# A fourth subtract level in the rounding chains of an SSM and ternary feed-forward layer

## The chip, the cores and the metric

The kernel runs on one Trainium2 chip, on 8 cores. Each core computes one of the 8 sequences of the batch with the same program and its own input; the cores exchange nothing. The time is the device time of the slowest core, in microseconds (us); lower is better. Engines are named as the profile names them: PE is TensorE, DVE is VectorE, ACT is ScalarE, POOL is GpSimd, SP is SyncE.

## The reference

For every sequence x of 4096 positions and 1024 features, the layer is, cut to what matters:

```python
u   = rmsnorm(layernorm(x));  Bu = u @ B_w.T            # 256 states
h_t = lam * h_(t-1) + Bu_t;   y  = h @ C_w.T + D_skip * u
a   = layernorm(x) + y;       z  = rmsnorm(a)
x   = x + a + (silu(z @ w1.T) * (z @ w3.T)) @ w2.T      # 2736 wide

def act_quant(v):                                       # per position
    scale = 127.0 / max(max(abs(v)), 1e-5)
    return clip(round(v * scale), -128, 127) / scale
def bitlinear(v, w, b):                                 # w in {-1, 0, 1} / scale
    return act_quant(rmsnorm2(v)) @ weight_quant(w).T + b
h   = gelu(bitlinear(layernorm(x), f1, b1))             # 4096 wide
x   = x + bitlinear(h, f2, b2)
```

What the change touches is the `round` in `act_quant`, once for the 1024 features that enter the first ternary product and once for the 4096 that enter the second.

## The kernel before, in words

Features lie on the partitions and positions along the free axis. A tile is 256 positions (TT), so a core has 16 tiles. Each phase goes over all 16 tiles.

**The order of the work.** There is no scheduler. `ctx.op` appends an instruction to its engine's list in the order in which the Python code runs, and works out which semaphore values it must wait for from the names that it reads and writes. Each engine takes its own list strictly in that order. An instruction that reads what the one before it on the same engine wrote waits for that engine's own semaphore too, so the instructions of a rounding chain come one after the other.

**First phase** (`p1_...`). Per tile: `p1_A` loads x and computes the statistics and the scan (L270 to L333). `p1_B` computes the state output and the second norm, and ends with the S1 tile (L374). `p1_CD` does the gated feed-forward: 22 slices with 8 matmuls for the gate (L390) and 8 for the value (L396), in three PSUM tiles PaA, PaB and PaC that are used in turn. ACT computes silu (L401) and DVE multiplies (L404), which frees two PSUM tiles; then 176 matmuls with w2 (L411). `p1_E` adds, stores the result to DRAM and computes the scale of `act_quant`. `p1_y1s` multiplies by it (L520). `p1_F` rounds, in 8 chunks of 128x256, and stores each chunk to DRAM (L548, L550). The loop runs `p1_CD(it)`, `p1_A(it+1)`, `p1_E(it)`, `p1_y1s(it)`, `p1_B(it+1)`, `p1_F(it)`. So on DVE the rounding of tile `it` lies behind the S1 tile of tile `it+1`, and ahead of the L404 multiplies of `it+1`.

**Weights.** Behind a barrier, the two ternary weight matrices are read twice from DRAM: once for the mean of their absolute values (L600 to L612), once to be made -1, 0 or 1 in bf16 (L650 to L664).

**Second phase** (`p2_...`). Per tile, column group by column group (fc, 32 of 128 columns): 8 matmuls into one of two PSUM tiles (L716), a multiplication by DVE that reads them (L723), GELU by ACT into HHT (L726), the square by ACT (L732), one matmul that sums the squares (L735), and two DVE instructions for the running maximum (L746, L749). `p2_stats` turns sum and maximum into the scale. `p2_quant_pair(it, g)` scales and rounds two column groups at a time, in 128x512 (L805 to L828), into HQT. `p2_m7_mms` does the 256 matmuls of the second product from HQT (L836), `p2_m7_evac` finishes the tile. The loop interleaves two tiles: for each pair g, DVE rounds pair g of tile `it`, and then the column groups 2g and 2g+1 of tile `it+1` are computed. The second product of tile `it-1` is put on PE ahead of that loop, and so is, for all tiles but the last, the broadcast of the next tile's scale into IABC (L152 on PE, L155 on DVE, called at L698), which DVE takes ahead of pair 0.

**The rounding chain.** DVE converts to int32 and back (L809, L811 and L529, L531) and subtracts, which leaves the fractional difference d (L813, L533). Then 4.0 is added (L816, L536), and for each s of 4, 2 and 1 a mask "d > s - 0.5" is computed (L820, L540) and s times the mask is subtracted (L824, L544). What is left is subtracted from the value (L828, L548). `round_chain` (L157) holds a third copy of the chain, but nothing calls it.

Of the kernel before, what the change touches and what calls it, by code (L numbers as in the profile page):

```python
# [106 lines left out]
def build(T=4096, TT=256):  # L107
# [38 lines left out]
           f=lambda e: e.dma_start(out=IDF[:], in_=identd[:]))  # L146
# [10 lines left out]
    def round_chain(src_ap, src_keys, iq, kiq, dbuf, kd, mask_ap, kmask, emit_out):  # L157
        ctx.op("dve", r=list(src_keys), w=[kiq],
               f=lambda e: e.tensor_copy(out=iq, in_=src_ap))
        ctx.op("dve", r=list(src_keys) + [kiq], w=[kd],  # L160
               f=lambda e: e.scalar_tensor_tensor(out=dbuf, in0=iq, scalar=-1.0,
                                                  in1=src_ap, op0=ALU.mult, op1=ALU.add))
        ctx.op("dve", r=[kd], w=[kd],
               f=lambda e: e.tensor_scalar(out=dbuf, in0=dbuf, scalar1=4.0,
                                           scalar2=None, op0=ALU.add))
        for s in (4.0, 2.0, 1.0):
            ctx.op("dve", r=[kd], w=[kmask],
                   f=lambda e, s=s: e.tensor_scalar(out=mask_ap, in0=dbuf,
                                                    scalar1=s - 0.5, scalar2=None,
                                                    op0=ALU.is_gt))  # L170
            ctx.op("dve", r=[kd, kmask], w=[kd],
                   f=lambda e, s=s: e.scalar_tensor_tensor(out=dbuf, in0=mask_ap,
                                                           scalar=-s, in1=dbuf,
                                                           op0=ALU.mult, op1=ALU.add))
        emit_out()
# [347 lines left out]
    def p1_F(it):  # L523
        t0 = it * TT
        X = X0 if it % 2 == 0 else X1
        kX = "X%d" % (it % 2)
        for c in range(NCHUNK):
            ctx.op("dve", r=[kX], w=["XI1"],
                   f=lambda e, c=c, X=X: e.tensor_copy(out=XI1[:], in_=X[:, c, :]))  # L529
            ctx.op("dve", r=["XI1"], w=["DHP"],  # L530
                   f=lambda e: e.tensor_copy(out=DHP[:], in_=XI1[:]))  # L531
            ctx.op("dve", r=[kX, "DHP"], w=["DHP"],
                   f=lambda e, c=c, X=X: e.tensor_tensor(out=DHP[:], in0=X[:, c, :],  # L533
                                                         in1=DHP[:], op=ALU.subtract))
            ctx.op("dve", r=["DHP"], w=["DHP"],
                   f=lambda e: e.tensor_scalar(out=DHP[:], in0=DHP[:], scalar1=4.0,  # L536
                                               scalar2=None, op0=ALU.add))
            for s in (4.0, 2.0, 1.0):
                ctx.op("dve", r=["DHP"], w=["MHP"],
                       f=lambda e, s=s: e.tensor_scalar(out=MHP[:], in0=DHP[:],  # L540
                                                        scalar1=s - 0.5, scalar2=None,
                                                        op0=ALU.is_gt))
                ctx.op("dve", r=["DHP", "MHP"], w=["DHP"],
                       f=lambda e, s=s: e.scalar_tensor_tensor(out=DHP[:], in0=MHP[:],  # L544
                                                               scalar=-s, in1=DHP[:],
                                                               op0=ALU.mult, op1=ALU.add))
            ctx.op("dve", r=[kX, "DHP"], w=["XQS"],
                   f=lambda e, c=c, X=X: e.tensor_tensor(out=XQS[:], in0=X[:, c, :],  # L548
                                                         in1=DHP[:], op=ALU.subtract))
            ctx.op("sp", r=["XQS"], w=["xqh"], dma="xq",  # L550
                   f=lambda e, c=c, t0=t0: e.dma_start(
                       out=xqh[c * 128:(c + 1) * 128, t0:t0 + TT], in_=XQS[:]))
# [248 lines left out]
    def p2_quant_pair(it, g):  # L801
# [11 lines left out]
               f=lambda e: e.tensor_tensor(out=DH[:], in0=Y1H[:], in1=DH[:],  # L813
                                           op=ALU.subtract))
        ctx.op("dve", r=["DH"], w=["DH"],
               f=lambda e: e.tensor_scalar(out=DH[:], in0=DH[:], scalar1=4.0,  # L816
                                           scalar2=None, op0=ALU.add))
        for s in (4.0, 2.0, 1.0):
            ctx.op("dve", r=["DH"], w=["MH"],
                   f=lambda e, s=s: e.tensor_scalar(out=MH[:], in0=DH[:],  # L820
                                                    scalar1=s - 0.5, scalar2=None,
                                                    op0=ALU.is_gt))
            ctx.op("dve", r=["DH", "MH"], w=["DH"],
                   f=lambda e, s=s: e.scalar_tensor_tensor(out=DH[:], in0=MH[:],  # L824
                                                           scalar=-s, in1=DH[:],
                                                           op0=ALU.mult, op1=ALU.add))
# [125 lines left out]
```

How the kernel before makes its waits and increments, by code:

```python
            def body(e):  # L892
                for o in ops:
                    for s, v in o.waits:
                        e.wait_ge(sem[s], v)
                    if o.emit is not None:
                        instr = o.emit(e)
                        instr.then_inc(sem[o.sem], o.inc)
```

## Time and profile before

| What | Value |
|---|---|
| Time, median of 2 runs | 7898.35 us (7889.26 to 7907.43) |
| The profiled execution | 7907.0 us |
| Its span on the slowest core, core 1 | 7905.4 us |
| Spans of the 8 cores | 7877.9 to 7905.4 us |
| DVE busy | 3924.4 us in 8881 instructions |
| PE busy | 3167.4 us in 19024 matmuls |
| ACT busy | 865.6 us in 1563 instructions |

The profile records one execution; its span is the time from the first to the last instruction of a core, and the execution's own time lies 1.6 us above it. Busy time is the sum over an engine's instructions. Idle time is counted ahead of an instruction and put down to what released it. The granted clock of PE is given as a share of 2.4 GHz.

### The profile page before, as it was taken

What the parts mean: (1) busy time and instruction counts of PE and PEld (TensorE: products, weight loads), DVE (VectorE), ACT (ScalarE), POOL (GpSimd) and SP (SyncE); (2) the same over time, 40 slices, a digit from 0 to 9 for tenths busy, and PEclk for the clock granted to TensorE, in tenths of its full rate; (3) what the DMA queues carried; (4) which work ended last, traced back from release to release, by engine and by line L of the source; (5) the groups of instructions that cost most, each with busy time, mean ns of one, the idle gap of its engine ahead of it and who ended that gap; (6) DMA issues with size and microseconds to landing.
All of it is one profiled execution on the core that took longest, in us unless ns stands there. A gap on an engine that the chain in (4) does not pass through costs nothing.

```text
span 7905.4 us, 65940 instructions; the slowest of 8 cores (7877.9 to 7905.4 us)
## 1 busy us (share of the span) xinstructions
PE 3167.4 (40%) x19024; PEld 2061.8 (26%) x19024; DVE 3924.4 (50%) x8881; ACT 865.6 (11%) x1563; POOL 5.1 (0%) x8
## 2 busy tenths in 40 slices
PE   3444444444444443300443444344443444344433
PEld 2333333333333332100221222122222222122212
DVE  2444454455445555443445544554455444544465
ACT  1000000001000000000211111111111111111110
POOL 0000000000000000000000000000000000000000
PEclk8666666666666666555555555555555555555556
DMA  6000000000000000522000000000000000000000
GB/s 105 14 14 14 14 14 14 14 14 18 15 14 14 14 14 11 171 106 74 8 1 14 14 14 0 14 14 14 9 5 14 14 14 1 14 14 14 1 11 11
DMA packets 120946, 173.91 MB, mean 22 GB/s; under 512 B 5748, under 2 KB 105236, under 8 KB 118548
## 3 DMA queue, kind: packets, MB, share of 16 engines
q1 hardware_dynamic: 115412, 152.20, 6.0%
q0 software_dynamic: 5184, 17.50, 1.4%
q8 instruction: 164, 2.69, 0.1%
q14 instruction: 186, 1.52, 0.1%
HBM read 145.22 MB, written 41.96 MB: 24 GB/s over the span
## 4 chain that ended last, share of the span: by engine, by line
DVE 44%; PE 30%; issue 12%; ACT 7%; DMA 5%; DVEq 2%; ACTq 0%; SPq 0%
DVE DH L824 7%; PE psH L716 6%; PE psO L836 6%; PE psF L411 4%; ACT HHT L726 4%; DVE MH L820 3%; DVE PR L723 3%; DMA WQ<-f2T 3%; DVE DHP L544 2%; DVEq L895 2%; PE psRow L260 2%; ACT HS L732 2%; PE PaC L152 1%; PE PaB L390 1%; PE PaA L390 1%
## 5 line engine op out<-in xcount | busy, mean ns | idle before, releaser
L735 PE MATMUL psRowH<-HS,ONEB 128*1 128x256 bf16 x512 | 190.1, 371 | 2223.9 <-ACT HS L732 2223.9
L716 PE MATMUL psH<-XQ,f1q 128*128 128x256 bf16 x4096 | 954.4, 414 | 10.8 <-DVE IABC L155 10.8
L735 PEld LDWEIGHTS psRowH<-HS,ONEB 128*1 128x1 bf16 x512 | 40.5, 79 | 2451.9 <-issue 2451.9
L716 PEld LDWEIGHTS psH<-XQ,f1q 128*128 128x128 bf16 x4096 | 525.8, 139 | 335.5 <-issue 148.1
L726 ACT ACTIVATE HHT<-PR,B1S,THR 128x256 f16<-128x256 f32 x512 | 306.8, 599 | 2621.2 <-DVE PR L723 2621.0
L824 DVE SCALAR_TENSOR_TENSOR DH<-MH,DH 128x512 f16<-128x512 f16 x768 | 531.6, 692 | 82.9 <-DVE MH L820 4.3
L836 PE MATMUL psO<-HQT,f2q 128*128 128x256 bf16 x4096 | 495.4, 285 | 119.1 <-DVE HQT L828 109.5
L723 DVE TENSOR_TENSOR PR<-psH,IABC 128x256 f32<-128x256 f32 x512 | 215.6, 421 | 593.8 <-PE psH L716 593.7
L836 PEld LDWEIGHTS psO<-HQT,f2q 128*128 128x128 bf16 x4096 | 412.7, 102 | 207.5 <-issue 145.3
L411 PE MATMUL psF<-GV,w2sb 128*128 128x256 bf16 (+1 forms) x2816 | 350.2, 279 | 21.3 <-DVE GV L404 11.8
L746 DVE TENSOR_TENSOR MX<-MX,HHT 128x256 f16<-128x256 f16 x496 | 145.3, 293 | 417.7 <-ACT HHT L726 417.7
L390 PE MATMUL PaB<-S1b,w1sb 128*128 128x256 bf16 x896 | 129.8, 293 | 484.3 <-DVE GV L404 484.3
L411 PEld LDWEIGHTS psF<-GV,w2sb 128*128 128x128 bf16 (+1 forms) x2816 | 270.2, 99 | 102.7 <-issue 63.9
L152 PE MATMUL PaC<-ROWS,ONESR 1*128 1x256 f32 x224 | 132.9, 694 | 353.0 <-DVE ROWS L310 113.3
L820 DVE TENSOR_SCALAR MH<-DH 128x512 f16<-128x512 f16 x768 | 225.9, 294 | 84.3 <-DVE DH L824 2.3
L749 DVE SCALAR_TENSOR_TENSOR MX<-HHT,MX 128x256 f16<-128x256 f16 x496 | 211.0, 425 | 53.0 <-DVE MX L746 1.9
L155 DVE CAST IABC<-psH 128x256 f16<-128x256 f32 x16 | 6.8, 425 | 452.5 <-PE psH L152 452.5
L152 PE MATMUL psH<-ROW,ONESR 1*128 1x256 f32 x96 | 50.0, 615 | 440.7 <-DMA ROW<-iah 363.6
L390 PEld LDWEIGHTS PaB<-S1b,w1sb 128*128 128x128 bf16 x896 | 91.9, 104 | 503.4 <-issue 488.2
L732 ACT ACTIVATE HS<-HHT 128x256 bf16<-128x256 f16 x512 | 213.2, 416 | 76.4 <-ACT HHT L726 2.1
L390 PE MATMUL PaA<-S1b,w1sb 128*128 128x256 bf16 (+1 forms) x1024 | 157.4, 305 | 89.1 <-DVE XI L529 83.4
L287 DVE TENSOR_SCALAR ROWS<-psRow 1x256 f32<-1x256 f32 x16 | 6.6, 412 | 362.0 <-PE psRow L260 362.0
(162 smaller groups left out, 4623.7 us busy)
## 6 DMA issues: line engine op xcount, KB each, us to landing
WQ<-f1T SPq DMA_DIRECT2D x16, 2048.0 KB, 7.8
WQ<-f2T SPq DMA_DIRECT2D x64, 512.0 KB, 3.5
X<-xT SPq DMA_DIRECT2D x16, 1024.0 KB, 5.7
xoh<-XOUT SPq DMA_DIRECT2D x16, 1024.0 KB, 4.4
XO<-xoh SPq DMA_DIRECT2D x16, 1024.0 KB, 8.6
outT<-FIN SPq DMA_DIRECT2D x16, 1024.0 KB, 5.6
xqh<-XQS SPq DMA_DIRECT2D x128, 64.0 KB, 1.6
XQ<-xqh SPq DMA_DIRECT2D x16, 512.0 KB, 9.5
```

The source lines that it names most:

```text
L152: f=lambda e: e.matmul(pgrp[:, 0:TT], ONESR[:], row_ap, start=True, stop=True))
L390: mm = e.matmul(pg[0:fsz, :], w1sb[:, c, off:off + fsz], S1[:, c, :], start=(c == 0), stop=(c == NCHUNK - 1))
L411: mm = e.matmul(psF[:, dc, :], w2sb[0:fsz, fs, dc * 128:(dc + 1) * 128], GV[0:fsz, fs, :], start=(fs == 0), stop=(fs == 21))
L716: mm = e.matmul(pH[:], f1q[:, c, fc * 128:(fc + 1) * 128], XQ[:, c, :], start=(c == 0), stop=(c == NCHUNK - 1))
L723: f=lambda e, pH=pH, PR=PR: e.tensor_tensor(out=PR[:], in0=pH[:], in1=IABC[:], op=ALU.mult))
L726: f=lambda e, fc=fc, PR=PR: e.activation(out=HHT[:, fc, :], in_=PR[:], func=AF.Gelu, bias=B1S[:, fc:fc + 1], scale=THR[:, 4:5]))
L732: f=lambda e, fc=fc, hsq=hsq: e.activation(out=hsq[:], in_=HHT[:, fc, :], func=AF.Square))
L735: f=lambda e, fc=fc, hsq=hsq: e.matmul(psRowH[:, 0, :], ONEB[:], hsq[:], start=(fc == 0), stop=(fc == F2CHUNK - 1)))
L749: f=lambda e, fc=fc: e.scalar_tensor_tensor(out=MX2[:], in0=HHT[:, fc, :], scalar=-1.0, in1=MX2[:], op0=ALU.mult, op1=ALU.max))
L820: f=lambda e, s=s: e.tensor_scalar(out=MH[:], in0=DH[:], scalar1=s - 0.5, scalar2=None, op0=ALU.is_gt))
L824: f=lambda e, s=s: e.scalar_tensor_tensor(out=DH[:], in0=MH[:], scalar=-s, in1=DH[:], op0=ALU.mult, op1=ALU.add))
L836: mm = e.matmul(psO[:, dc, :], f2q[0:128, fc, dc * 128:(dc + 1) * 128], HQT[:, fc, :], start=(fc == 0), stop=(fc == F2CHUNK - 1))
```

## The change

The rounding chain starts from 8.0 instead of 4.0, and has four levels (8, 4, 2, 1) instead of three. Each chain gets two DVE instructions more: a compare and a scalar_tensor_tensor. The edit stands in three places.

```diff
@@ round_chain
-               f=lambda e: e.tensor_scalar(out=dbuf, in0=dbuf, scalar1=4.0,
+               f=lambda e: e.tensor_scalar(out=dbuf, in0=dbuf, scalar1=8.0,
                                            scalar2=None, op0=ALU.add))
-        for s in (4.0, 2.0, 1.0):
+        for s in (8.0, 4.0, 2.0, 1.0):
...
@@ p1_F
-                   f=lambda e: e.tensor_scalar(out=DHP[:], in0=DHP[:], scalar1=4.0,
+                   f=lambda e: e.tensor_scalar(out=DHP[:], in0=DHP[:], scalar1=8.0,
                                                scalar2=None, op0=ALU.add))
-            for s in (4.0, 2.0, 1.0):
+            for s in (8.0, 4.0, 2.0, 1.0):
                 ctx.op("dve", r=["DHP"], w=["MHP"],
                        f=lambda e, s=s: e.tensor_scalar(out=MHP[:], in0=DHP[:],
                                                         scalar1=s - 0.5, scalar2=None,
...
@@ p2_quant_pair
-               f=lambda e: e.tensor_scalar(out=DH[:], in0=DH[:], scalar1=4.0,
+               f=lambda e: e.tensor_scalar(out=DH[:], in0=DH[:], scalar1=8.0,
                                            scalar2=None, op0=ALU.add))
-        for s in (4.0, 2.0, 1.0):
+        for s in (8.0, 4.0, 2.0, 1.0):
             ctx.op("dve", r=["DH"], w=["MH"],
                    f=lambda e, s=s: e.tensor_scalar(out=MH[:], in0=DH[:],
                                                     scalar1=s - 0.5, scalar2=None,
```

The order of DVE changes in two places; that of the other engines doesn't. In the second phase, DVE's list for the rounding of one pair and what follows it stood so before (DH holds the difference, MH the mask, HQT the rounded value, psH0 the PSUM tile of the next tile's column group):

```order
L813 TENSOR_TENSOR DH<-Y1H,DH 128x512 [waits dve]
L816 TENSOR_SCALAR DH<-DH 128x512 [waits dve]
L820 TENSOR_SCALAR MH<-DH 128x512 [waits dve]
L824 SCALAR_TENSOR_TENSOR DH<-MH,DH 128x512 [waits dve]
L820 TENSOR_SCALAR MH<-DH 128x512 [waits dve]
L824 SCALAR_TENSOR_TENSOR DH<-MH,DH 128x512 [waits dve]
L820 TENSOR_SCALAR MH<-DH 128x512 [waits dve]
L824 SCALAR_TENSOR_TENSOR DH<-MH,DH 128x512 [waits dve]
L828 TENSOR_TENSOR HQT<-Y1H,DH 128x512 [waits dve]
L723 TENSOR_TENSOR PR0<-psH0,IABC 128x256 [waits pe]
```

And so stands DVE's list at the same place of the changed kernel:

```order
L813 TENSOR_TENSOR DH<-Y1H,DH 128x512 [waits dve]
L816 TENSOR_SCALAR DH<-DH 128x512 [waits dve]
L820 TENSOR_SCALAR MH<-DH 128x512 [waits dve]
L824 SCALAR_TENSOR_TENSOR DH<-MH,DH 128x512 [waits dve]
L820 TENSOR_SCALAR MH<-DH 128x512 [waits dve]
L824 SCALAR_TENSOR_TENSOR DH<-MH,DH 128x512 [waits dve]
L820 TENSOR_SCALAR MH<-DH 128x512 [waits dve]
L824 SCALAR_TENSOR_TENSOR DH<-MH,DH 128x512 [waits dve]
L820 TENSOR_SCALAR MH<-DH 128x512 [waits dve]
L824 SCALAR_TENSOR_TENSOR DH<-MH,DH 128x512 [waits dve]
L828 TENSOR_TENSOR HQT<-Y1H,DH 128x512 [waits dve]
L723 TENSOR_TENSOR PR0<-psH0,IABC 128x256 [waits pe]
```

One compare and one scalar_tensor_tensor stand between the difference and the rounded value, and the read of the PSUM tile is two instructions further down.

In the first phase, DVE's list for one chunk of p1_F stood so before (XI1 is the int32 value, DHP the difference, MHP the mask, XQS the rounded chunk):

```order
L529 CAST XI1<-X0 128x256
L531 CAST DHP<-XI1 128x256
L533 TENSOR_TENSOR DHP<-X0,DHP 128x256
L536 TENSOR_SCALAR DHP<-DHP 128x256
L540 TENSOR_SCALAR MHP<-DHP 128x256
L544 SCALAR_TENSOR_TENSOR DHP<-MHP,DHP 128x256
L540 TENSOR_SCALAR MHP<-DHP 128x256
L544 SCALAR_TENSOR_TENSOR DHP<-MHP,DHP 128x256
L540 TENSOR_SCALAR MHP<-DHP 128x256
L544 SCALAR_TENSOR_TENSOR DHP<-MHP,DHP 128x256
```

In the changed kernel DVE has at this place:

```order
L529 CAST XI1<-X0 128x256
L531 CAST DHP<-XI1 128x256
L533 TENSOR_TENSOR DHP<-X0,DHP 128x256
L536 TENSOR_SCALAR DHP<-DHP 128x256
L540 TENSOR_SCALAR MHP<-DHP 128x256
L544 SCALAR_TENSOR_TENSOR DHP<-MHP,DHP 128x256
L540 TENSOR_SCALAR MHP<-DHP 128x256
L544 SCALAR_TENSOR_TENSOR DHP<-MHP,DHP 128x256
L540 TENSOR_SCALAR MHP<-DHP 128x256
L544 SCALAR_TENSOR_TENSOR DHP<-MHP,DHP 128x256
L540 TENSOR_SCALAR MHP<-DHP 128x256
L544 SCALAR_TENSOR_TENSOR DHP<-MHP,DHP 128x256
```

Here too each chunk is two instructions longer. DVE's list has 768 rows more in all: 2 for each of the 128 chunks of the first phase and of the 256 pairs of the second.

## Rows read from the trace of the kernel before

**Rows 1.** The page, part 1 (busy us, share, instructions); the spans and clocks by core.

```profile
PE 3167.4 (40%) x19024; PEld 2061.8 (26%) x19024; DVE 3924.4 (50%) x8881; ACT 865.6 (11%) x1563; POOL 5.1 (0%) x8
...
core 1: 7905.4 us, clock 0.604
...
core 4: 7877.9 us, clock 0.607
```

**Rows 2.** Windows of core 1: busy us (instructions) by engine, PEclk, DMA share, GB/s.

```profile
0.00:3180.00 3180.00, 1430.89 (x9904) 1027.82 (x9904) 1526.78 (x3607) 297.88 (x491) 5.15 (x8) 0.68 0.08 20
...
3870.00:7878.00 4008.00, 1583.63 (x8398) 954.09 (x8399) 2112.75 (x4988) 532.21 (x1005) 0.00 (x0) 0.56 0.03 10
```

**Rows 3.** The page, part 4: the chain that ended last.

```profile
DVE 44%; PE 30%; issue 12%; ACT 7%; DMA 5%; DVEq 2%; ACTq 0%; SPq 0%
DVE DH L824 7%; PE psH L716 6%; PE psO L836 6%; PE psF L411 4%; ACT HHT L726 4%; DVE MH L820 3%; DVE PR L723 3%; DMA WQ<-f2T 3%; DVE DHP L544 2%; DVEq L895 2%; PE psRow L260 2%; ACT HS L732 2%; PE PaC L152 1%; PE PaB L390 1%; PE PaA L390 1%
```

**Rows 4.** Groups of DVE: busy us, mean ns | idle us before, releasers.

```profile
L824 DVE SCALAR_TENSOR_TENSOR DH<-MH,DH 128x512 f16<-128x512 f16 x768 | 531.6, 692 | 82.9 <-DVE MH L820 4.3
L820 DVE TENSOR_SCALAR MH<-DH 128x512 f16<-128x512 f16 x768 | 225.9, 294 | 84.3 <-DVE DH L824 2.3 <-DVE DH L816 1.7
...
L544 DVE SCALAR_TENSOR_TENSOR DHP<-MHP,DHP 128x256 f16<-128x256 f16 x384 | 163.3, 425 | 42.2 <-DVE MHP L540 2.6
...
L540 DVE TENSOR_SCALAR MHP<-DHP 128x256 f16<-128x256 f16 x384 | 87.2, 227 | 43.3 <-DVE DHP L544 2.3 <-DVE DHP L536 0.9
```

**Rows 5.** Waits: who waited for whom, us in total, times, longest us.

```profile
PE psRowH L735 <- ACT HS L732: 2223.9, 512, 15.5
...
DVE PR L723 <- PE psH L716: 593.7, 272, 2.6
...
PE PaB L390 <- DVE GV L404: 484.3, 15, 33.3
...
DVE IABC L155 <- PE psH L152: 452.5, 16, 32.0
```

**Rows 6.** Timeline of one pair, second phase: start, us, instruction, idle before.

```profile
5088.06 0.42 DVE L723 TENSOR_TENSOR PR<-psH,IABC 128x256 f32<-128x256 f32 x1
...
5094.54 1.89 PE L716 MATMUL psH<-XQ,f1q 128*128 128x256 bf16 x8
...
5097.24 0.69 DVE L824 SCALAR_TENSOR_TENSOR DH<-MH,DH 128x512 f16<-128x512 f16 x1
5098.04 0.29 DVE L820 TENSOR_SCALAR MH<-DH 128x512 f16<-128x512 f16 x1
5098.44 0.69 DVE L824 SCALAR_TENSOR_TENSOR DH<-MH,DH 128x512 f16<-128x512 f16 x1
...
5100.43 0.42 DVE L828 TENSOR_TENSOR HQT<-Y1H,DH 128x512 bf16<-128x512 f16 x1
5100.77 0.42 DVE L723 TENSOR_TENSOR PR<-psH,IABC 128x256 f32<-128x256 f32 x1
...
5103.00 1.89 PE L716 MATMUL psH<-XQ,f1q 128*128 128x256 bf16 x8
```

**Rows 7.** Timeline of DVE, pair 0 of the last tile, second phase.

```profile
7731.43 0.69 DVE L824 SCALAR_TENSOR_TENSOR DH<-MH,DH 128x512 f16<-128x512 f16 x1
7757.14 0.42 DVE L828 TENSOR_TENSOR HQT<-Y1H,DH 128x512 bf16<-128x512 f16 x1 [25.02 <-PE psO L836]
```

**Rows 8.** Windows, first phase: L411 in two tiles, and the chain of p1_F.

```profile
2306.00:2332.00 26.00, 25.40 (x180) 18.55 (x181) 0.94 (x1) 1.22 (x1) 0.00 (x0) 0.81 0.00 1
...
2882.00:2904.00 22.00, 21.40 (x179) 16.80 (x180) 0.99 (x1) 1.28 (x1) 0.00 (x0) 1.00 0.01 1
...
2996.00:3034.00 38.00, 5.37 (x34) 3.94 (x33) 28.68 (x89) 2.05 (x3) 0.00 (x0) 0.59 0.04 13
```

**Rows 9.** L836 on the timeline, and the window of the pairs behind it.

```profile
5131.53 5.81 PE L836 MATMUL psO<-HQT,f2q 128*128 128x256 bf16 x32
5137.49 7.15 PE L836 MATMUL psO<-HQT,f2q 128*128 128x256 bf16 x64
...
5167.00:5391.00 224.00, 72.03 (x289) 36.19 (x290) 131.81 (x311) 35.48 (x67) 0.00 (x0) 0.50 0.04 12
```

## Prediction

> **What bounds the kernel now.** I read the page first, for the busy shares [rows 1]: VectorE (DVE) is busy for 3924.4 us of a span of 7905.4, TensorE for 3167.4. Neither is near full, so the shares alone name no bound. The stage windows [rows 2] split the span into three parts: the first phase (16 tiles, 0 to 3180 us), the weight passes, and the second phase (16 tiles, 3870 to 7878 us). The chain that ended last [rows 3] gives 44% of the span to DVE and 30% to TensorE, and its largest line is L824, one of the two instructions that the change adds: the engines take turns, and time added in a DVE turn counts in full unless TensorE would have been the later one there. So the question is who waits for whom around the two rounding chains.
>
> In the second phase, the timeline of one pair of column groups [rows 6] answers it. TensorE does the next 8 matmuls of L716 from 5094.54 to 5096.43 us, beneath the DVE chain. DVE goes through its three levels and starts L828 only at 5100.43. The read of that PSUM tile (L723) follows at 5100.77 with no wait, since the matmuls had been done for 4.3 us. Only the second chunk's matmuls, 5103.00 to 5104.89, make DVE wait, and they can't start before the first chunk has gone through L723, GELU and square, all behind the chain. The waits say the same for all tiles [rows 5]: DVE waits at L723 for TensorE 272 times, so for about one chunk of each pair; TensorE waits for the square (L735 behind L732) for 2223.9 us in all. The rounding chain is in series with everything else in the pair.
>
> In the first phase, the chain of lines 529 to 548 stands on DVE ahead of the L404 multiplies of the next tile. TensorE fills its three PSUM tiles and then stands still until the first L404 frees one: 484.3 us in 15 waits, 32.3 us each [rows 5]. The window from 2996 to 3034 us shows that stretch, with TensorE busy for 5.37 of 38 us [rows 8]. So this chain is in series too.
>
> **The change, part by part.** The constant 4.0 that becomes 8.0 changes no instruction's shape, and costs nothing. Each chain gets a fourth level: one compare (L820 or L540) and one scalar_tensor_tensor (L824 or L544), with operands and shapes that the trace already has three times per chain. The edit of round_chain is in a function that nothing calls. So no price is unknown; each is read from the same lines [rows 4]. Since every one of these instructions waits for the one before it on its own engine, the idle time ahead of them belongs to the price.
>
> - Second phase, one level over 128x512 f16: L824 takes 531.6 us busy and 82.9 idle, L820 takes 225.9 busy and 84.3 idle, 924.7 us over 768 of each, 1.204 us. The timeline agrees: from one L824 to the next it is 1.20 us [rows 6]. There are 16 tiles with 16 pairs, 256 levels more.
> - Of these 256, one is covered. In tile 15 no input of a next tile is loaded, so DVE starts pair 0 at once, and L828 then waits 25.02 us for the 256 matmuls of the tile before, which read the buffer that it writes [rows 7]. In the other tiles DVE waits for those matmuls ahead of the chain, at the cast of IABC (452.5 us in 16 waits [rows 5]), so pair 0's chain comes after them and is exposed. 255 x 1.204 = 307.0 us.
> - First phase, one level over 128x256 f16: (163.3 + 42.2 + 87.2 + 43.3) / 384 = 0.875 us. 16 tiles with 8 chunks: 128 x 0.875 = 112.0 us. All of it is exposed, the last tile too, where a barrier stands behind the chain. The DMA that empties XQS, a single buffer, gets more time from one chunk to the next with the fourth level, not less.
>
> At these two places the Trainium skill has a rule on the gap. Measured: L820 starts 0.80 us behind the start of an L824 that takes 0.69, a gap of 0.11 [rows 6]. "VectorE: DVE Perf Modes", section "The DRAIN you can't avoid", puts a pipeline flush of about the operation's duration less 266 ns behind each operation. With the means of rows 4 a level of 512 would then take 294 + 28 + 692 + 426 = 1440 ns, one of 256 would take 227 + 425 + 159 = 811 ns, and the change would cost 367 + 104 = 471 us. The trace doesn't bear the rule out for this pair, and the measured gap decides.
>
> The sum is 307.0 + 112.0 = 419.0 us. The profiled execution took 7907.0 us for a span of 7905.4, so it would become 8326. It lies 8.65 us above the median of the runs, 7898.35; I forecast from the median: 7898.35 + 419.0 = 8317 us, 5.3% more.
>
> Two things can move this beside the added work, and both are TensorE's clock. First, its cold start. In the 256 matmuls of a tile (L836) the first 32 take 5.81 us where 64 take 7.15 later [rows 9], so 5.81 - 3.58 = 2.2 us are lost before it has risen to 2.4 GHz. Each tile of either phase has one such start, 32 in all, and I take the first phase's for as dear. The longer tiles shift where the clock rises. If the loss vanished or doubled in all of them it would be 70 us less or more; but as some tiles will gain where others lose, I take 0, and 10 us to each side. Beyond that a longer DVE stretch can't cool TensorE: it is at 0.50 (1.2 GHz) all through the pairs already [rows 9]. Second, a level between the two. The 176 matmuls of L411 fill a window of 22 us at granted clock 1.00 (2.4 GHz), and one of 26 us at 0.81 [rows 8]. Core 1, the slowest, shows it; between the slowest and the fastest core lie 27.5 us at otherwise equal work [rows 1]. I take no change, with 27 us to each side as the far ends. Of an instruction stream that grows by 768 of DVE's 8881 instructions, the means in rows 4 already hold the occasional longer gap (1.204 against the usual 1.20).
>
> **Rivals.**
> 1. The 0.81 level goes. TensorE rests longer between its dense blocks, so whatever brings 0.81 may come less often. The slowest core would then be like the fastest: 8317 - 27 = 8290 us. For it: the stretches at 0.81 are all in dense blocks of the first phase. Against it: the dense blocks themselves are as long as before. The Trainium skill, "TensorE: Matmul & The Clock Gate", has such a level of 13/16 as a peak-current limit when three cores of a die run dense matmuls (section "Seeing it yourself"); 0.81 in rows 8 agrees with it, and by it the level would come back in the same blocks, so that the time stays at the forecast. Chance of rival 1: 0.05. The mirror of it, more tiles at 0.81, costs 4 us per tile in L411; in 13 tiles more it would be 52 us, 8369 us. Chance 0.03.
> 2. Only the second phase pays. If TensorE's three blocks ahead of the stall in the first phase grew or DVE's chain ended before TensorE needs it, 112 us would be hidden: 7898 + 307 = 8205 us. Against it stand the 32.3 us of wait per tile, which the chain would have to lose before it were covered. Chance 0.02.
> 3. Not slower. The place is the pair loop and the mechanism TensorE as the later one: the added level lies beneath the matmuls of the next chunk, and L723 starts as before. It decides as soon as those matmuls end later than L828 does, which needs 4.3 us more of them, over three times their 1.89. With the first phase beneath its matmuls too, the time stays at 7898 us. The idle 50% of DVE speaks for it at first sight; that L723 starts directly behind L828 in rows 6 speaks against it. Chance 0.02.
> 4. The change doesn't do what it says, if the compiled program drops or merges a level. Against it: the order of the changed kernel holds 768 more DVE rows, and four compares in each chain. The time would be 7898 us; its chance is counted with rival 3.
>
> **How the numbers follow.** The forecast as worked out has 0.87. With 10 us for cold starts and part of the 27 us of the 0.81 level its own range is 8295 to 8341, and I give that as the whole range: what is left out (rivals 2 to 4, the far parts of rival 1, an error of mine in the sum) is under 2 in 10. A measurement of this kernel can tell about 2% from no change, 158 us. Slower by over 2%: the forecast and rivals 1 and 2, 0.97. Within 2%: rivals 3 and 4, 0.02. Faster by over 2%: nothing in the rows gives it, 0.01.
>
> **What would show it right or wrong.** In the profile of the changed kernel L820 and L824 should have 1024 instructions each at 294 and 692 ns, L540 and L544 512 each at 227 and 425 ns, DVE busy for 3924.4 + 256 x 0.986 + 128 x 0.652 = 4260 us, and TensorE's busy time unchanged. The wait of PE PaB L390 for L404 should grow from 32.3 to about 39 us, that of L828 for psO should shrink from 25.0 to 23.8 us, and a pair should take 1.2 us more than its 12.7 (from L723 at 5088.06 to L723 at 5100.77 in rows 6). The waits of L723 for TensorE should stay at 272 times and 594 us. If they shrink by much, the chain was covered in part (rivals 2 and 3). If the added gaps are longer than 0.11 us, the price per level was wrong. If the added lines fit and the total doesn't, it is the clock: the windows of L411 and L836 would show it.

## The result, and the profile after

The changed kernel takes 8358.44 us (median of 11 runs, 8336.40 to 8404.92). Beside it the kernel before takes 7910.09 us (median of 10, 7886.50 to 7927.98). The ratio is 1.0579, with a 95% interval from 1.0555 to 1.0603. An execution in which one die is over 1% longer than the other at a lower granted clock is left out of the median times below (8019.84 us in experiment 5, 7553.66 us in experiment 12). The forecast was 8317 us in a range from 8295 to 8341, so the direction and the main term held, but the time lies 17 us above the range. Of the 41 us between forecast and result, 12 lie in the base (two runs had a median of 7898.35, ten have 7910.09). The other 29 lie in the difference: 448 us, where 419 were forecast.

Part 1 of the page of the changed kernel, slowest core, answers to [rows 1]:

```profile
PE 3216.3 (38%) x19024; PEld 2085.4 (25%) x19024; DVE 4261.8 (51%) x9649; ACT 865.6 (10%) x1563; POOL 5.2 (0%) x8
```

DVE has its 768 instructions more and is busy for 4261.8 us, against the 4260 worked out. TensorE is busy for 49 us more, with the same instructions: that is already a sign of its clock.

The groups of DVE on core 4 of the changed kernel (busy us, mean ns | idle us before) answer to [rows 4]:

```profile
L824 DVE SCALAR_TENSOR_TENSOR DH<-MH,DH 128x512 f16<-128x512 f16 x1024 | 709.0, 692 | 112.0 <-DVE MH L820 7.7
L820 DVE TENSOR_SCALAR MH<-DH 128x512 f16<-128x512 f16 x1024 | 300.9, 294 | 112.0 <-DVE DH L824 3.7 <-DVE DH L816 0.9
L544 DVE SCALAR_TENSOR_TENSOR DHP<-MHP,DHP 128x256 f16<-128x256 f16 x512 | 217.7, 425 | 56.2 <-DVE MHP L540 3.4
...
L540 DVE TENSOR_SCALAR MHP<-DHP 128x256 f16<-128x256 f16 x512 | 116.2, 227 | 56.9 <-DVE DHP L544 2.8 <-DVE DHP L536 0.5
```

A level costs (709.0 + 112.0 + 300.9 + 112.0) / 1024 = 1.205 us in the second phase and (217.7 + 56.2 + 116.2 + 56.9) / 512 = 0.873 us in the first. The forecast had 1.204 and 0.875.

The waits on the slowest core, core 3, answer to [rows 5] (us in total, times, longest us):

```profile
PE psRowH L735 <- ACT HS L732: 2514.9, 512, 16.7
...
DVE PR L723 <- PE psH L716: 594.1, 272, 2.6
...
PE PaB L390 <- DVE GV L404: 582.5, 15, 39.6
...
DVE IABC L155 <- PE psH L152: 451.9, 16, 32.3
```

DVE's wait at L723 is what it was, 272 times and 594 us, so nothing of the added levels was absorbed there. TensorE waits 582.5 / 15 = 38.8 us per tile for the first L404 instead of 32.3; the forecast was about 39. The one covered pair shows too. In the timeline of core 4, pair 0 of the last tile, the wait of [rows 7] is 24.17 us long instead of 25.02. The forecast was 23.8, 1.2 us less:

```profile
8151.87 0.43 DVE L828 TENSOR_TENSOR HQT<-Y1H,DH 128x512 bf16<-128x512 f16 x1 [24.17 <-PE psO L836]
```

So the missing 29 us are not in the chains. To find them, compare cores whose TensorE clock was hardly ever at 0.81. Core 4 of the changed kernel has 11 us at 0.81, and in experiment 1, the kernel before once more, core 4 has none. These are the windows of core 4 of the changed kernel, cut at its stages: the first phase, the weight pass for the mean (first L603 to the end of the last), the pass that makes the ternary weights (first L654 to the end of the last L662), and the second phase. The first number behind the stretch is its length in us, then busy us by engine, PEclk, DMA share, GB/s:

```profile
88.60:3251.30 3162.70, 1411.67 (x9888) 1018.37 (x9888) 1609.93 (x3856) 292.08 (x481) 0.82 (x1) 0.67 0.06 15
3264.20:3458.60 194.40, 59.78 (x252) 26.54 (x252) 75.49 (x43) 0.00 (x0) 0.00 (x0) 0.54 0.49 162
3473.80:3823.10 349.30, 0.00 (x0) 0.00 (x0) 160.37 (x120) 0.00 (x0) 0.00 (x0) 0.50 0.27 90
3831.10:8314.50 4483.40, 1675.57 (x8854) 1006.76 (x8854) 2411.68 (x5615) 567.83 (x1072) 0.00 (x0) 0.56 0.03 9
```

The same stages on core 4 of the kernel before, in experiment 1:

```profile
91.10:3141.30 3050.20, 1409.62 (x9888) 1017.05 (x9888) 1527.07 (x3600) 292.41 (x481) 0.91 (x1) 0.68 0.06 16
3152.50:3331.60 179.10, 59.08 (x252) 26.33 (x252) 75.53 (x43) 0.00 (x0) 0.00 (x0) 0.55 0.51 176
3346.20:3687.90 341.70, 0.00 (x0) 0.00 (x0) 160.41 (x120) 0.00 (x0) 0.00 (x0) 0.50 0.27 92
3695.60:7869.50 4173.90, 1673.72 (x8854) 1005.93 (x8854) 2160.42 (x5103) 567.94 (x1072) 0.00 (x0) 0.56 0.03 10
```

The first phase is 112.5 us longer (forecast 112.0) and the second 309.5 (forecast 307.0). But the two weight passes take 543.7 us instead of 520.8, with the same DVE work of 236 us in them and the same bytes. Nothing in the passes was edited, and they begin behind a barrier, so the longer chains ahead of them only shift their start. That is the term that the prediction didn't have.

### The profile page after: what moved, and what is told of

The parts are those of the page before. It is cut to its first block, busy times and chain, and to the rows that moved or that the text cites. A ratio compares the mean times of both kernels' runs of the same rounds, so it can differ in the third digit from the quotient of the medians.

```text
span 8396.0 us, 67476 instructions; the slowest of 8 cores (8319.7 to 8396.0 us)
## 1 busy us (share of the span) xinstructions
PE 3216.3 (38%) x19024; PEld 2085.4 (25%) x19024; DVE 4261.8 (51%) x9649; ACT 865.6 (10%) x1563; POOL 5.2 (0%) x8
## 4 chain that ended last, share of the span: by engine, by line
DVE 45%; PE 29%; issue 12%; ACT 7%; DMA 5%; DVEq 2%; ACTq 0%; SPq 0%
DVE DH L824 9%; PE psH L716 6%; PE psO L836 6%; PE psF L411 4%; ACT HHT L726 4%; DVE MH L820 4%; DMA WQ<-f2T 3%; DVE DHP L544 3%; DVE PR L723 3%; DVEq L895 2%; PE psRow L260 2%; ACT HS L732 1%; DVE MHP L540 1%; PE PaB L390 1%; PE PaC L396 1%
## 5 line engine op out<-in xcount | busy, mean ns | idle before, releaser
L824 DVE SCALAR_TENSOR_TENSOR DH<-MH,DH 128x512 f16<-128x512 f16 x1024 | 708.8, 692 | 112.1 <-DVE MH L820 7.7
L836 PE MATMUL psO<-HQT,f2q 128*128 128x256 bf16 x4096 | 494.4, 284 | 137.4 <-DVE HQT L828 127.9
L723 DVE TENSOR_TENSOR PR<-psH,IABC 128x256 f32<-128x256 f32 x512 | 215.8, 422 | 594.2 <-PE psH L716 594.1
L836 PEld LDWEIGHTS psO<-HQT,f2q 128*128 128x128 bf16 x4096 | 412.4, 102 | 225.1 <-issue 163.6
L411 PE MATMUL psF<-GV,w2sb 128*128 128x256 bf16 (+1 forms) x2816 | 361.9, 285 | 21.7 <-DVE GV L404 12.2
L390 PE MATMUL PaB<-S1b,w1sb 128*128 128x256 bf16 x896 | 135.5, 302 | 582.5 <-DVE GV L404 582.5
L820 DVE TENSOR_SCALAR MH<-DH 128x512 f16<-128x512 f16 x1024 | 301.3, 294 | 112.0 <-DVE DH L824 3.7
L411 PEld LDWEIGHTS psF<-GV,w2sb 128*128 128x128 bf16 (+1 forms) x2816 | 275.2, 101 | 109.9 <-issue 65.8
L152 PE MATMUL PaC<-ROWS,ONESR 1*128 1x256 f32 x224 | 132.9, 695 | 350.4 <-DVE ROWS L310 112.0
L544 DVE SCALAR_TENSOR_TENSOR DHP<-MHP,DHP 128x256 f16<-128x256 f16 x512 | 217.8, 425 | 56.2 <-DVE MHP L540 3.4
L390 PEld LDWEIGHTS PaB<-S1b,w1sb 128*128 128x128 bf16 x896 | 94.7, 107 | 604.2 <-issue 586.4
```

The lines of the kernel that those rows point to most:

```text
L390: mm = e.matmul(pg[0:fsz, :], w1sb[:, c, off:off + fsz], S1[:, c, :], start=(c == 0), stop=(c == NCHUNK - 1))
L411: mm = e.matmul(psF[:, dc, :], w2sb[0:fsz, fs, dc * 128:(dc + 1) * 128], GV[0:fsz, fs, :], start=(fs == 0), stop=(fs == 21))
L723: f=lambda e, pH=pH, PR=PR: e.tensor_tensor(out=PR[:], in0=pH[:], in1=IABC[:], op=ALU.mult))
L820: f=lambda e, s=s: e.tensor_scalar(out=MH[:], in0=DH[:], scalar1=s - 0.5, scalar2=None, op0=ALU.is_gt))
L836: mm = e.matmul(psO[:, dc, :], f2q[0:128, fc, dc * 128:(dc + 1) * 128], HQT[:, fc, :], start=(fc == 0), stop=(fc == F2CHUNK - 1))
```

## The experiments

In the tables below "passes" is the length of the two weight passes together, cut as above, as the median of the 8 cores of a profile; "first phase" and "second phase" are cut the same way, and given for the core where it is shortest. "Fastest core" is the median, over all executions of a kernel, of the shortest span among its 8 cores. It keeps most of the 0.81 clock out, which as a rule lengthens only some cores. Experiments 1 to 4, 5 to 8, 9 to 11, and 12 ran on four different chips. The fastest core of the kernel before took 7877.0, 7876.9, 7876.2 and 7876.4 us on them, so the experiments can be compared.

**Experiments 1 and 2: both kernels once more.** No edit.

> The kernel before, once more, so that its cores can be seen in several executions. In the profiles the changed kernel's core 4, which had almost no time at granted clock 0.81, is 441.8 us longer than core 4 before, not 419: 111.7 in the first phase and 307.5 in the second as summed, and 23 us more in the weight passes (520.5 us before, 543.7 after, both passes together). Theory A (weight passes vary from execution to execution, whatever the kernel): the two passes of the least disturbed core lie anywhere from 515 to 550 us here. Theory B (the passes are slower because of something the change does): 517 to 527 us here, as in the first profile. Time 7890 to 7925 us in both.

> The changed kernel, once more. Theory A (weight passes vary by chance): the two passes of the least disturbed core lie anywhere from 515 to 550 us. Theory B (a lasting effect of the change): 538 to 550 us again. Theory C (the cores that are slowest are so by the 0.81 clock in the first phase): the first phase is 3163 us (+-3) on cores with under 40 us at 0.81, and longer by 0.13 us for each us at 0.81 on the others. Time 8336 to 8400 us in all.

| | Time, median | Fastest core | First phase | Passes | Second phase | us at 0.81, by core |
|---|---|---|---|---|---|---|
| before, first profile | 7910.09 | | 3049 | 524.1 | 4171 | 33 to 170 |
| e1, before | 7901.64 | 7878.1 | 3048 | 523.9 | 4171 | 0 on all |
| change, first profile | 8358.44 | 8319.2 | 3163 | 547.2 | 4481 | 11 to 485 |
| e2, change | 8339.88 | 8317.6 | 3162 | 547.8 | 4480 | 0 to 90 |

Theory A fell. The passes are not longer by chance: the 16 cores of the two profiles of the kernel before lie between 520.5 and 527.0 us, the 16 of the changed kernel between 540.5 and 555.9. The fastest cores differ by 8319.2 - 7878.1 = 441 us, which is 419 and some 23 of the passes. Theory C held in part: in the first profile of the changed kernel core 3 has 485 us at 0.81 and a first phase of 3225.0 us, core 4 has 11 and 3162.7, so each us at 0.81 costs (3225.0 - 3162.7) / (485 - 11) = 0.13 us. The windows of one tile at each clock, on core 3, show the price where it is paid (the second row has the tile at full clock):

```profile
731.00:939.00 208.00, 99.36 (x617) 68.71 (x615) 100.48 (x240) 18.20 (x30) 0.00 (x0) 0.62 0.04 13
1948.00:2146.00 198.00, 89.27 (x618) 64.31 (x618) 100.69 (x242) 18.19 (x30) 0.00 (x0) 0.66 0.05 14
```

A tile lasts 208 us with its dense blocks at 0.81 and 198 us without, with the same DVE work. TensorE's busy time makes up the 10 us. But the time at 0.81 differs from one execution to the next more than between the kernels: the kernel before had 33 to 170 us of it in one profile and none in the other.

**Experiments 3 and 4: one half of the change each.** Experiment 3 keeps the edit of p2_quant_pair alone, experiment 4 that of p1_F alone:

```diff
 # e3: p1_F stays as it was
-        for s in (4.0, 2.0, 1.0):            # p2_quant_pair, with scalar1=8.0 at L816
+        for s in (8.0, 4.0, 2.0, 1.0):
 # e4: p2_quant_pair stays as it was
-            for s in (4.0, 2.0, 1.0):        # p1_F, with scalar1=8.0 at L536
+            for s in (8.0, 4.0, 2.0, 1.0):
```

> The fourth level in p2_quant_pair alone; p1_F keeps three. The sum of the prediction gives +307 us. First phase 3050 us on undisturbed cores as before, second phase 4481 us against 4172. Theory B1 (the weight passes are slower because the longer first phase changes when the cores get there): the passes stay at 520 us, time about 7910 + 307 = 8217 us. Theory B2 (they are slower through the longer program or anything else in it): 538 us or more, time about 8235 us. Theory C: the stretches at 0.81 are as few as before, so the spread of the cores stays near 27 us.

> The fourth level in p1_F alone; p2_quant_pair keeps three. The sum gives +112 us: first phase 3163 us on undisturbed cores, second phase 4172 us as before. Theory B1: the weight passes take 538 us or more, and the time is 7910 + 112 + 20 (passes) and some 10 to 20 more for the clock = 8045 to 8060 us. Theory A: the passes lie anywhere from 515 to 550 us, and the time at 8022 to 8050. Theory C: as many stretches at 0.81 as in the changed kernel (over 200 us on the slowest core).

| | Time, median | Ratio (95%) | Fastest core | Passes |
|---|---|---|---|---|
| before, same executions | 7891.89 | | 7877.0 | 523.9 |
| e3, second phase only | 8221.48 | 1.0407 (1.0383 to 1.0432) | 8200.2 | 539.8 |
| e4, first phase only | 8020.22 | 1.0148 (1.0119 to 1.0177) | 7994.6 | 527.3 |
| e2, the whole change | 8339.88 | 1.0559 (1.0535 to 1.0584) | 8317.6 | 547.8 |

On the fastest cores the halves cost 323.2 and 117.6 us, together 440.8, and the whole costs 440.6: they add. Each is, within 3 us, the forecast term (307 and 112) plus its part of the passes (16 and 3). This tells the theories apart. The first-phase edit comes ahead of the passes and hardly moves them; the second-phase edit comes behind them and makes them 16 us longer. So theory B1 (when the cores arrive) fell, and what is left is something of the program as a whole, B2. In experiment 4 every core had 207 to 292 us at 0.81 in its profile, in experiment 3 at most 75; with one profile each I draw nothing from it.

**Experiments 5, 6 and 7: a longer program without a longer chain.** They leave the rounding as it was. Experiments 5 and 6 add 1024 one-element memsets on DVE or GpSimd at the same place of the code, and experiment 7 adds a DRAM tensor. DVE does them from 1 to 47 us, while the first weights load. GpSimd has the weight loads ahead of them in its list, so it does them from 97 to 142 us, beneath the first tile.

```diff
 # e5 ("dve") and e6 ("pool"), ahead of the L238 loop
+    for k in range(1024):
+        ctx.op("dve", w=["XQS"] if k == 1023 else [],
+               f=lambda e, k=k: e.memset(XQS[32 * (k // 256):32 * (k // 256) + 1,
+                                             k % 256:k % 256 + 1], 0.0))
 # e7
+    padh = dram("padh", [128, 128], F32, "Internal")
...
+    ctx.op("pool", r=["IDF"], w=["padh"], dma="wc",
+           f=lambda e: e.dma_start(out=padh[:], in_=IDF[:]))
```

> The kernel before with 1024 one-element memsets on DVE while the first weights load (DVE sits idle there until about 90 us), so that DVE's program is longer by about as much as the change makes it, with the same rounding. So far the two weight passes took 521 to 527 us in both profiles of the kernel before and 524 to 530 with the first-phase edit alone, 534 to 543 with the second-phase edit alone and 541 to 556 in the changed kernel, although nothing ahead of or in the passes differs. Theory P (the longer program, by what it shifts in DRAM or by its fetching): passes of 534 us or more here. Theory Q (something only the second phase's edit does): 520 to 528 us. The first phase stays at 3050 us and the second at 4172 us on undisturbed cores in both.

> The kernel before with the same 1024 one-element memsets on GpSimd instead, at the same place. If any longer program slows the weight passes (theory P, placement in DRAM), they take 534 us or more here too. If only DVE's own instruction stream matters (theory P2, fetching), they stay at 520 to 528 us while e5 is slow. Theory Q: 520 to 528 us in both.

> The kernel before with one more DRAM tensor of 64 KB, written once at the start by a GpSimd DMA. It shifts what the DRAM holds and leaves all programs but for that one DMA. Theory P in its placement form: the weight passes can move from 524 us, to 534 or more or to less than 518. Theories P2 and Q: 520 to 528 us.

The two passes of core 4, experiment 5 (DVE padding):

```profile
3159.50:3344.40 184.90, 59.60 (x252) 26.39 (x252) 75.47 (x43) 0.00 (x0) 0.00 (x0) 0.54 0.51 170
3361.40:3714.70 353.30, 0.00 (x0) 0.00 (x0) 160.47 (x120) 0.00 (x0) 0.00 (x0) 0.50 0.27 89
```

The two passes of core 4, experiment 6 (GpSimd padding):

```profile
3144.80:3323.30 178.50, 59.59 (x252) 26.35 (x252) 75.55 (x43) 0.00 (x0) 0.00 (x0) 0.54 0.52 177
3338.10:3681.30 343.20, 0.00 (x0) 0.00 (x0) 160.47 (x120) 0.00 (x0) 0.00 (x0) 0.50 0.27 92
```

The same memsets make the passes of core 4 538.2 us long on DVE and 521.7 on GpSimd. Over all cores the medians are 541.5 us in experiment 5, 524.9 in experiment 6 and 523.4 in experiment 7. The rounding is the old one in all three. So it is the length of DVE's program that lengthens the passes, not what the change computes, and neither a longer GpSimd program nor 64 KB more in DRAM does it. Whether those 64 KB shifted anything else in DRAM no run shows.

The fastest core is 7891.8 us in experiment 5 against 7876.9 of the kernel before. In the time of the slowest core the 0.81 clock blurs that: the median is 7913.76 us against 7902.86, and the ratio 1.0010 (0.9994 to 1.0026). Experiment 6 takes 7883.38 us (ratio 0.9977, 0.9947 to 1.0007) and experiment 7 7913.36 (1.0029, 0.9997 to 1.0061).

Experiment 6 brought something that I had not expected: its first phase is 3038 us at best instead of 3048, its second 4162 instead of 4171, and its fastest core 7861.9 us.

**Experiment 8: one level less.** The sum must also hold downwards.

```diff
-                                            scalar1=4.0, ...          # L164, L536, L816
+                                            scalar1=2.0, ...
-        for s in (4.0, 2.0, 1.0):                                     # L166, L538, L818
+        for s in (2.0, 1.0):
```

> One level fewer than before in both chains (offset 2.0, levels 2 and 1). If a level costs what the sum says, the time falls by the same 419 us: first phase 3050 - 112 = 2938 us and second phase 4172 - 307 = 3865 us on undisturbed cores, time about 7892 - 419 = 7473 us with passes at 524 us. Theory P (a shorter program can also be faster or slower): the weight passes may differ by 10 to 25 us. A rival: with one level less, TensorE or ACT becomes the later one somewhere, and the gain stays under 380 us.

It takes 7456.45 us, ratio 0.9437 (0.9419 to 0.9456). Its median first phase is 2937.0 us and its second 3864.5, against 3049.9 and 4172.8 in experiment 1: 112.9 and 308.3 us less. The passes take 510.4 us, 13.5 less, which is most of the 17 us by which the time lies under the expected 7473. The rival that another engine takes over fell: TensorE is still waited for at L723 272 times, for 595.5 us on core 4. This version is faster than both kernels.

**Experiments 9 and 10: how much, and which program.** Experiment 9 adds 2048 memsets on DVE instead of 1024, experiment 10 adds 512 one-column matmuls with their weight loads on TensorE, at the same place.

```diff
 # e9
+    for k in range(2048):
+        T_ = XQS if k < 1024 else GBH
+        ctx.op("dve", f=lambda e, k=k % 1024, T_=T_: e.memset(
+            T_[32 * (k // 256):32 * (k // 256) + 1, k % 256:k % 256 + 1], 0.0))
 # e10
+    def emit_pad(e):
+        for k in range(512):
+            mm = e.matmul(psF[0:1, 7, 0:1], ONEB[:], ONEB[:], start=True, stop=True)
+        return mm
+    ctx.op("pe", r=["onesbf"], w=[kF(7)], f=emit_pad)
```

> The kernel before with 2048 one-element memsets on DVE at the start, twice those of e5. The medians of the two weight passes so far, by what DVE's program has more or less: one level less 510, nothing 524, first-phase edit 527, second-phase edit 540, 1024 memsets 541.5, the whole change 547.5 us. If the passes go with the length of DVE's program (theory P2), they take 553 to 562 us here; if there was one step between two lengths, 540 to 548. The start of the first phase may come some 35 us later, since DVE isn't free at 90 us.

> The kernel before with 512 one-column matmuls (and their 512 weight loads) on TensorE at the start, where it sits idle. Theory P2a (DVE's program alone counts): weight passes at 522 to 528 us. Theory P2b (the program of any engine that is read from DRAM counts, but GpSimd's didn't): 535 to 545 us.

| Kernel | DVE's program against before | KB on the instruction queues, against before | Passes, median of 8 cores |
|---|---|---|---|
| e8 | a level less | -96 | 510.4 |
| before, e1 | | 0 | 523.9 |
| e4 | 256 instructions more, each with its wait | +32 | 527.3 |
| e3 | 512 more, each with its wait | +64 | 539.8 |
| e5 | 1024 memsets more | +64 | 541.5 |
| the change | 768 more, each with its wait | +96 | 547.2 and 547.8 |
| e9 | 2048 memsets more | +128 | 555.6 |
| e6, e7 | as before (GpSimd or DRAM padded) | +64, 0 | 524.9, 523.4 |
| e10 | as before (TensorE padded) | +64 | 541.5 |

The third column comes from the packets of the two DMA queues that the profile calls instruction: q14, whose packets have 8 KB, and q8, whose packets have 16 KB and which alone grew in experiment 10. These are the lines of q14 (packets, MB, share) on core 4, first experiment 1, then 5, then 6:

```profile
q14 instruction: 186, 1.52, 0.1%
q14 instruction: 194, 1.59, 0.1%
q14 instruction: 194, 1.59, 0.1%
```

The passes grow with DVE's program, by some 17 us for 1024 memsets and another 14 for the next 1024. By KB the rows fall into line: 3 us for 32 KB, 16 to 18 for 64 (levels, memsets or matmuls), 24 for 96, 32 for 128. Theory P2a fell: TensorE's program counts just as DVE's does, with 541.5 us for its 1024 instructions. Of the three engines tried, GpSimd alone doesn't count: its program takes the same 64 KB more, for 1 us. And the passes have no more fetching inside them than before: on core 4 of experiments 1, 5, 6, 8 and 9 and of the changed kernel 6 packets of q14 and 2 of q8 start in their windows, 0.08 MB beside 65 MB of weights.

Experiment 9's time was 7937.05 us (ratio 1.0029, 1.0001 to 1.0057). Its memsets ended at 94 us, so the first phase started only 5 us later, not 35. Experiment 10's time was 8017.39 us in 2 runs (ratio 1.0142, 1.0090 to 1.0195); its profile has 83 to 1023 us at 0.81, which explains its longer first phases (up to 3190.7 us), but not why there was so much of it.

**Experiments 11 and 12: the GpSimd memsets with the change, and with one level less.** The edit is that of experiment 6, on the changed kernel and on experiment 8.

> The changed kernel with the 1024 GpSimd memsets of e6. In e6 these left the weight passes alone (525 us), yet made the first phase 9 us and the second 8 us shorter; on one core the gaps of 0.46 us in DVE's chains fell from 49 to 19. If that was the memsets' doing, both phases are shorter here too (3155 and 4475 us on undisturbed cores, against 3163 and 4483) and the passes stay at 547 us; time 8320 to 8340 against 8340 to 8358. If it was chance, nothing changes. The added levels cost 307 + 112 us in both.

> One level less than before (e8) and the 1024 GpSimd memsets (e6), the fastest pair of edits so far. If the two add up, the first phase is 2937 - 9 = 2928 us and the second 3864.5 - 9 = 3855 us, with weight passes at 510 us, and the time is about 7456 - 19 = 7437 us. If the memsets' effect was chance, 7456 us.

Experiment 11 took 8316.9 us, ratio 1.0525 (1.0497 to 1.0553), its fastest core 8284.4 us against 8317.6 in experiment 2. Its phases have medians of 3152.5 and 4467.1 us against 3163.9 and 4483.9 in experiment 2, and its passes 543.5, where 547 were expected. Experiment 12 has undisturbed phases of 2930 and 3853 us, and passes of 510.2. So the shortening came three times out of three. It is no chance: on the fastest core, not one execution with the memsets is as long as the shortest of the same kernel without them (7856.6 to 7873.8 us against 7874.0 and more in the kernel before beside it, 8282.7 to 8297.6 against 8311.8 and more, 7424.5 to 7431.8 against 7438.4 and more).

Experiment 12 took 7436.80, 7437.21 and 7468.14 us, a median of 7437.21, as expected (7437), against 7456.45 in experiment 8. As 7468.14 is above all four executions of experiment 8, the gain isn't shown for the slowest core. It is the fastest version of all that were run.

## Why the prediction was right or wrong, point by point

**What bounds the kernel: right.** Both chains are in series with the rest. The waits that would have absorbed an added level kept their size (L723: 272 times, 594.1 us), and the one that the chain causes grew as forecast (38.8 us per tile at L390).

**The price of a level and the number of exposed ones: right.** 1.205 and 0.873 us were measured for 1.204 and 0.875. On core 4 the first phase grew by 112.5 us and the second by 309.5, for 112.0 and 307.0. The single covered pair was covered, with 24.17 us of wait left for the 23.8 forecast. Experiments 3, 4 and 8 confirm both terms apart from each other and with the other sign. The gap of 0.11 us held too, so the larger flush that the Trainium skill's "VectorE: DVE Perf Modes" (section "The DRAIN you can't avoid") would put there was rightly set aside; by it the estimate was 471 us in all, and the two phases grew by 422.

**The step that failed: "Two things can move this beside the added work, and both are TensorE's clock".** There is a third, and it was the larger. The prediction looked at the longer instruction stream, but only for gaps within the chains, and said that the means of [rows 4] hold it already. They do. What it left out is that the weight passes, which wait for DRAM reads of two 4096 x 1024 matrices, each read twice, became 23 us longer. The prediction had no term at all for a stage without edits. The issues of DMA on core 4 show where the 23 us come from (KB each, median us from issue to landing). First the changed kernel:

```profile
WQ<-f1T SPq DMA_DIRECT2D x16, 2048.0 KB, 8.4
WQ<-f2T SPq DMA_DIRECT2D x64, 512.0 KB, 3.6
```

Then the kernel before, in experiment 1:

```profile
WQ<-f1T SPq DMA_DIRECT2D x16, 2048.0 KB, 7.7
WQ<-f2T SPq DMA_DIRECT2D x64, 512.0 KB, 3.4
```

These are 80 loads in a row, each 0.2 to 0.7 us later: 16 x 0.7 + 64 x 0.2 = 24 us by these medians, the size of what was missing. Added up load by load, from issue to landing, they take 373.2 us on core 4 instead of 346.4; the windows above show 22.9 of these 26.7 us, since they leave out the first load of each pass, and the gaps between the loads became 1.7 us shorter. Each is issued only when the one before it has landed, since `ctx.op` makes a DMA wait for the last one on its queue (L56), so the lateness adds up. In the second phase the loads of XO and XQ are later too (9.1 and 10.0 us against 8.2 and 9.2), but no instruction waits for them there. Nor do they follow the program's length: with a level less, in experiment 8, they take 9.6 and 11.0 us.

**The clock: the mechanism right, the sizes too small.** The 0.81 level is what separates the slowest core from the fastest. I took 27 us to each side, from a single profile. The profile of the changed kernel has 8396.0 - 8319.7 = 76 us between its cores. As a cost of the change it isn't settled: the slowest core lies 42 us above the fastest in the median of the changed kernel's 12 executions, and 21 us in the 4 of experiment 2; in the 22 executions of the kernel before beside experiments 5 to 8 it is 24 us.

The Trainium skill ("TensorE: Matmul & The Clock Gate", section "Seeing it yourself") says that this limit takes a whole die. The profile of the changed kernel agrees, though the totals of one die differ: cores 2 and 3 have 452 and 485 us at 0.81, cores 0 and 1 have 265 and 261. Core 0 enters the level at 373.3, 584.3, 793.3, 1000.0 and 1208.7 us of its span, in the midst of its dense blocks, and core 2 at 152.9, 363.8, 572.9, 779.6 and 988.3 us of its own, each time 220.4 or 220.5 us less. So the two enter it at the same moments, and core 0 had begun some 220 us earlier; the totals differ because the level shows only where a core's own dense block is. Cores 0 and 1 enter within 0.2 us of each other.

In the profile of the kernel before, the same comparison gives 3597.3 us, with core 2 ahead: core 0 enters at 737.3, 1521.6 and 2302.2 us, core 2 at 4334.6, 5118.9 and 5899.6. These three stretches of core 2 are in the L836 matmuls of its second phase, so the remark of rival 1 that the level is all in the first phase holds for core 1, but not for the chip. In experiment 4 the distance is 946.6 us. That the dense blocks of a die overlap more or less, as its cores start nearer or further apart, would make the level come and go between executions; it is a reading, and no run set the starts.

The cold starts cost nothing that can be seen: the second phase, with 16 of them, came out 2.5 us off the sum.

**The base.** 12 us of the miss are that the median of two runs was taken for the kernel's time, when single executions of the kernel before, beside experiments 1 to 4, lie anywhere from 7885 to 7960 us. With 7910, the 419 and the 23 the forecast would have been 8352. The 6 us that are then left aren't in the fastest cores, which differ by 441; they lie in the spread between cores.

**The rivals.** None of the four came about. Rival 1 and its mirror both lie within what executions do by chance: in the first profile of the changed kernel core 3's first phase is 62 us longer than core 4's, as the mirror would have it, and in experiment 2 no core has over 90 us at 0.81. Rivals 2 and 3 are excluded by the waits.

**What stays open.** Why a longer program of DVE or TensorE makes DRAM reads land later. The runs show that it isn't the work, the arrival time of the cores, 64 KB more data in DRAM, the program of GpSimd, or more instruction packets within the passes. They don't tell whether it is where the programs lie or push other things in DRAM, or something else in how they are fetched, and no run here moved a program without making it longer.

## What to carry to other kernels

For instructions that wait for each other on one engine, busy and idle time of their group over its count is a price that can be trusted: it was right to 0.002 us for a level up and held for a level down. A forecast must also ask what a longer program does to the stages that nobody edits, above all to those that run on a chain of DRAM loads with one in flight; here 768 instructions more cost them 4%, a twentieth of the whole effect. And when single cores differ by 27 us in a profile, the base needs more than two runs, and the fastest cores should be compared with each other before the slowest.

## What the runs showed of the hardware that I had not expected

- DRAM loads land later with a longer DVE or TensorE program: 510.4, 523.9, 541.5 and 555.6 us for the same two weight passes with a level less, with the old program, and with 1024 and 2048 memsets more. They follow the KB on the instruction queues over the whole run (96 less, as before, 64 and 128 more), but GpSimd's 64 KB don't count.
- 1024 one-element memsets on GpSimd at the start make both phases shorter, by 9 and 8 us in the medians with the old chains and by 11 and 17 with the changed ones. In the chains of core 4 (L531 to L544 and L809 to L824), gaps of over 0.2 us, most of them 0.46, where 0.10 is usual, come 49 times in the kernel before and 19 times with the memsets (58 and 20 with the change). By an estimate, 30 gaps with 0.36 us less each are 11 of the 17 us. What these longer gaps are, and why they go, wasn't tried.
- The granted clock of 0.81 comes and goes between executions of one kernel: 33 to 170 us by core in one profile of the kernel before, none on any core in another. Experiment 10 had up to 1023 us on a core.
- Two pairs of cores of one die enter the 0.81 level at the same moments, but at quite different places of their own spans: 220 us apart in the profile of the changed kernel, 3597 us in that of the kernel before, 947 us in experiment 4.
